# Layer 2's score products for the exponentials: four heads together, one key block by one query block

## The reference

```python
q = (x @ Wq).reshape(b, t, H, D)            # H = 16 heads, D = 64 = 32 "nope" + 32 rope
kv = kv_latent @ Wkvb                       # latent of 16 numbers per position
k = concat(kv, rope(k_rope))                # the rope part is one for all heads
v = concat(kv, zeros)
att = softmax(where(causal, q @ k.T / sqrt(D), -inf))
y = att @ v
x = x + y @ Wo
```

## Time and profile before

| | |
|---|---|
| median of 3 runs | 669.34 us (667.24 to 671.93) |
| profiled execution, its own time | 671.58 us |
| its span in the trace | 669.9 us |
| PE busy | 580.0 us (87%) |
| PEld busy | 342.0 us |
| DVE busy | 403.6 us (60%) |
| ACT busy | 311.2 us (46%) |
| POOL busy | 211.8 us (32%) |
| mean granted TensorE clock | 0.928 |

### The profile page before, as it was taken

One profiled execution on the slowest core, in us unless ns is written; L12 is line 12 of the kernel. 1 busy time (PEld: TensorE's weight loads), 2 busy tenths in 40 slices (PEclk: granted clock), 3 DMA queues, 4 the chain that ended last, 5 costly groups with the idle time before them and its releaser, 6 DMA issues.

```text
span 669.9 us, 10427 instructions
## 1 busy us (share of the span) xinstructions
PE 580.0 (87%) x3801; PEld 342.0 (51%) x3826; DVE 403.6 (60%) x932; ACT 311.2 (46%) x589; POOL 211.8 (32%) x276
## 2 busy tenths in 40 slices
PE   3884999887979899899978998999999998999873
PEld 1732444434434465555435555655676556654732
DVE  6374887676675655665675576756656764544362
ACT  2311756575453763456435545644445441553221
POOL 4562453242442622551252111405222002211101
PEclk9675999999988899899888999999999999999787
DMA  9322113111353433201570122225305020000000
GB/s 260 103 94 93 41 49 112 55 58 60 119 119 58 104 91 126 114 34 64 96 191 33 55 49 48 43 71 143 70 10 104 18 42 1 18 2 0 1 16 16
DMA packets 26658, 46.57 MB, mean 70 GB/s; under 512 B 3216, under 2 KB 12336, under 8 KB 26032
## 3 DMA queue, kind: packets, MB, share of 16 engines
q1 hardware_dynamic: 26608, 45.91, 25.0%
HBM read 27.62 MB, written 17.83 MB: 68 GB/s over the span
## 4 chain that ended last, share of the span: by engine, by line
PE 61%; DVE 15%; SPq 6%; DMA 5%; ACT 5%; issue 4%; POOL 4%; POOLq 0%; DVEq 0%; ACTq 0%
PE ps L541 13%; PE ps L605 11%; PE ps L509 10%; PE ps L483 6%; DVE NM L1098 4%; PE ps L485 4%; PE ps L480 3%; PE ps L507 3%; PE ps L726 2%; PE ps L655 2%; DVE stats L1082 2%; PE ps L549 2%; SPq L432 2%; DMA KS<-scr_k 1%; PE ps L588 1%
## 5 line engine op out<-in xcount | busy, mean ns | idle before, releaser
L1098 DVE TENSOR_REDUCE NM<-ps 128x1 f32<-128x512 f32 (+3 forms) x352 | 219.0, 637 | 126.6 <-PE ps L485 119.5
L764 ACT ACTIVATE PA<-ps 128x512 f32<-128x512 f32 x256 | 146.2, 595 | 148.7 <-PE ps L509 76.4
L509 PE MATMUL ps<-QS,K 128*128 128x384 f32 (+3 forms) x512 | 122.6, 353 | 0.0
L485 PE MATMUL ps<-maskb,identb 128*128 128x128 bf16 x512 | 111.1, 235 | 0.0
L509 PEld LDWEIGHTS ps<-QS,K 128*128 128x128 f32 x512 | 80.9, 191 | 39.7 <-issue 20.4
L1054 POOL TENSOR_SCALAR_AFFINE_SELECT PA<-PA 128x512 f32<-128x512 f32 x96 | 59.9, 637 | 123.8 <-ACT PC L768 123.3
L483 PE MATMUL ps<-K,QS 96*128 96x256 f32 (+3 forms) x256 | 88.2, 389 | 9.5 <-DVE NM L1098 9.2
L480 PE MATMUL ps<-KS,QS 96*128 96x256 bf16 (+3 forms) x256 | 74.2, 325 | 24.7 <-DVE NM L1098 16.4
L541 PE MATMUL ps<-PA,V 128*32 128x512 f32 (+2 forms) x768 | 80.1, 491 | 8.5 <-POOL PA L1054 7.6
L1012 POOL TENSOR_TENSOR whole<-terms 128x512 f32<-128x512 f32 x28 | 35.6, 1271 | 107.4 <-DVEq L1191 105.8
L957 POOL TENSOR_TENSOR rstd<-ve,half 128x4 f32<-128x4 f32 x20 | 20.4, 1020 | 154.6 <-DVE ve L1090 119.2
(11 more groups left out here) (156 smaller groups left out, 726.4 us busy)
## 6 DMA issues: line engine op xcount, KB each, us to landing
scr<-QC SPq DMA_DIRECT2D x24, 512.0 KB, 2.9
QS<-scr SPq DMA_DIRECT2D x32, 256.0 KB
QS<-scr_q SPq DMA_DIRECT2D x16, 288.0 KB
KS<-scr_k SPq DMA_DIRECT2D x16, 288.0 KB
QS<-scr SPq DMA_DIRECT2D x64, 64.0 KB
scr_k<-room SPq DMA_DIRECT2D x20, 128.0 KB, 1.9
scr_q<-room SPq DMA_DIRECT2D x12, 128.0 KB, 1.9
x<-in_x SPq DMA_DIRECT2D x4, 256.0 KB, 6.5
```

The source lines that it names most:

```text
L485: return pe.matmul(dst[:, P * (k - 1):P * k], identb[:], maskb[:, 0, :], start=False, stop=True)
L509: mm = pe.matmul(dst, keys[:, SEQ[n] % 2, q0:q0 + P], QS2[:, h, q0:T], start=(keys is K1), stop=(keys is K2))
L764: act.activation(PA[:, h % 8, T * k:T * k + T], ps[:, ST0 + (u + k) % 3, :], ACT.Exp, scale=scale)\
L1098: dve.tensor_reduce(dst, src, AX.X, ALU.max, negate=True).then_inc(fill_read, 1)
```

## The change

Layer 2's units become one pair (key block j, query block i) for the four heads of the group at once: two products of 512 columns (K1 and K2), whose moving operand is four pieces of 128 queries, one per head, 512 elements apart in QS2 (`scores_t2`). There are ten pairs with j at or below i, so there are still ten units; `BLOCKS2` takes the four diagonal ones first. Layer 1's units keep their shape (`scores_t1`).

The tiles PA and PC become one tile PG of two halves with ten places of 512 elements; `unit_place` says where a unit's exponential goes. In layer 2 the places are ordered so that for one head and one key block the query blocks lie 512 elements apart, and `values` reads its moving operand in 4, 3, 2 or 1 pieces of 128; its columns and its count are those of before. `values` waits once more, for all ten exponentials, and in layer 2 for all four causal instructions of its group.

POOL's causal instructions of layer 2 (`causal_blocks2`) are now one for each diagonal unit, 128 x 512 in one piece, stand at place (n, 2) instead of (n + 1, 0), and each waits only for its own unit's exponential.

The diff, without the views of constants that share the tile's memory:

```diff
@@ -40,6 +40,17 @@
 UNITS = 10
 
 CAUSAL_ORDER = (0, 1, 2, 3)
+
+BLOCKS2 = ((0, 0), (1, 1), (2, 2), (3, 3), (0, 1), (0, 2), (0, 3), (1, 2), (1, 3), (2, 3))
+PLACE2 = (0, 4, 7, 9)
+
+
+def unit_place(layer, c):
+    if layer == 2:
+        j, i = BLOCKS2[c]
+        return PLACE2[j] + i - j
+    hh, k = 2 * (c // 5) + (c % 5) // 2, (c % 5) % 2
+    return 8 + c // 5 if c % 5 == 4 else 2 * hh + k
 
 
 PHASES = ((1, 0), (1, 1), (1, 2), (2, 0), (1, 3), (2, 1), (2, 2), (2, 3))
@@ -262,8 +273,7 @@
         MRest = sb("MRest", [P, NT, HG])
         MF = sb("MF", [P, NT, 2, HG], F32R)
         MP = sb("MP", [3 * HG, 2, T])
-        PA = sb("PA", [P, 8, 2 * T])
-        PC = sb("PC", [P, 4, 2, 256])
+        PG = sb("PG", [P, 2, UNITS, T])
         OT = sb("OT", [P, T])
         rec = sb("rec", [P, NT, HG])
         ON1 = sb("ON1", [P, NT, H * D1])
...
@@ -500,14 +509,17 @@
                     mm = products(bank[:, w * j:w * j + w], n, h - heads + 1 + j, 3 - i, 4 - i)
                 mm.then_inc(score_fill, 1)
 
-            def scores_t(dst, n, h, j):
+            def scores_t1(dst, h, j):
 
                 q0 = P * j
-                if LAYER[n] == 1:
-                    return pe.matmul(dst, KS1[:, h, q0:q0 + P], QS1[:, h, q0:T], start=True, stop=True)
+                return pe.matmul(dst, KS1[:, h, q0:q0 + P], QS1[:, h, q0:T], start=True, stop=True)
+
+            def scores_t2(bank, n, j, i):
+
+                heads = slice(HG * (n % G), HG * (n % G) + HG)
                 for keys in (K1, K2):
-                    mm = pe.matmul(dst, keys[:, SEQ[n] % 2, q0:q0 + P], QS2[:, h, q0:T], start=(keys is K1),
-                                   stop=(keys is K2))
+                    mm = pe.matmul(bank.rearrange("p (h q) -> p h q", h=HG), keys[:, SEQ[n] % 2, P * j:P * j + P],
+                                   QS2[:, heads, P * i:P * i + P], start=(keys is K1), stop=(keys is K2))
                 return mm
 
             def scores_for_exp(n, hh, i):
@@ -519,27 +531,37 @@
                 if u >= 3:
                     pe.wait_ge(exp_done, u - 2)
                 bank = ps[:, ST0 + u % 3, :]
-                tiles = (((0, T, h, 0),), ((0, 3 * P, h, 1), (3 * P, T, h, 3)), ((0, 256, h - 1, 2), (256, T, h, 2)))[i]
-                for lo, hi, head, j in tiles:
-                    mm = scores_t(bank[:, lo:hi], n, head, j)
+                if LAYER[n] == 2:
+                    mm = scores_t2(bank, n, *BLOCKS2[u % UNITS])
+                else:
+                    tiles = (((0, T, h, 0),), ((0, 3 * P, h, 1), (3 * P, T, h, 3)),
+                             ((0, 256, h - 1, 2), (256, T, h, 2)))[i]
+                    for lo, hi, head, j in tiles:
+                        mm = scores_t1(bank[:, lo:hi], head, j)
                 mm.then_inc(st_ready, 1)
 
             def values(n, j):
 
-                pe.wait_ge(causal, NT * n + CAUSAL_ORDER.index(j) + 1)
+                pe.wait_ge(causal, NT * (n + 1) if LAYER[n] == 2 else NT * n + CAUSAL_ORDER.index(j) + 1)
                 if j == 0:
+                    pe.wait_ge(exp_done, UNITS * (n + 1))
                     if n:
                         pe.wait_ge(on_ready, n)
                     if n % G == 0:
                         pe.wait_ge(v1_ready if LAYER[n] == 1 else v2_ready, SEQ[n] + 1)
                 for hh in range(HG):
                     h = HG * (n % G) + hh
-                    slot = h % 8
-                    p = (PA[:, slot, 0:T], PA[:, slot, T:T + 3 * P], PC[:, slot // 2, hh % 2, :],
-                         PA[:, slot, T + 3 * P:2 * T])[j]
-                    v = V1[:, j, h, :] if LAYER[n] == 1 else V2[:, SEQ[n] % 2, j, :]
-                    mm = pe.matmul(ps[32 * hh:32 * hh + 32, BK_O, P * j:T], v, p, start=(j == 0), stop=(j == NT - 1),
-                                   skip_group_check=True)
+                    out = ps[32 * hh:32 * hh + 32, BK_O, P * j:T]
+                    if LAYER[n] == 1:
+                        v = V1[:, j, h, :]
+                        p = (PG[:, n % 2, 2 * hh, :], PG[:, n % 2, 2 * hh + 1, 0:3 * P],
+                             PG[:, n % 2, 8 + hh // 2, 256 * (hh % 2):256 * (hh % 2) + 256],
+                             PG[:, n % 2, 2 * hh + 1, 3 * P:T])[j]
+                    else:
+                        v = V2[:, SEQ[n] % 2, j, :]
+                        out = out.rearrange("d (i q) -> d i q", q=P)
+                        p = PG[:, n % 2, PLACE2[j]:PLACE2[j] + NT - j, P * hh:P * hh + P]
+                    mm = pe.matmul(out, v, p, start=(j == 0), stop=(j == NT - 1), skip_group_check=True)
                 if j == NT - 1:
                     mm.then_inc(pv, 1)
 
@@ -752,20 +774,15 @@
         def _(act):
             def main(n, hh):
                 if 0 <= n < NG:
-                    h = HG * (n % G) + hh
                     u = n * UNITS + 5 * (hh // 2) + 2 * (hh % 2)
                     scale = (D1 if LAYER[n] == 1 else D2) ** -0.5
                     if hh == 0 and n >= 2:
                         act.wait_ge(pv, n - 1)
                     if n <= 1 and hh == 0:
                         act.wait_ge(consts_ready, WCO if n else CONSTS)
-                    for k in range(2):
+                    for k in range(2 + hh % 2):
                         act.wait_ge(st_ready, u + k + 1)
-                        act.activation(PA[:, h % 8, T * k:T * k + T], ps[:, ST0 + (u + k) % 3, :], ACT.Exp, scale=scale)\
-                           .then_inc(exp_done, 1)
-                    if hh % 2:
-                        act.wait_ge(st_ready, u + 3)
-                        act.activation(PC[:, (h % 8) // 2, :, :].rearrange("p a t -> p (a t)"), ps[:, ST0 + (u + 2) % 3, :],
+                        act.activation(PG[:, n % 2, unit_place(LAYER[n], (u + k) % UNITS), :], ps[:, ST0 + (u + k) % 3, :],
                                        ACT.Exp, scale=scale).then_inc(exp_done, 1)
                 if hh == 2 and 1 <= n <= NG:
                     act.wait_ge(pv, n)
@@ -1043,20 +1060,28 @@
                 pool.wait_ge(q_low, c + 1)
                 pool.sem_inc(job_done[j], 1)
 
-            def causal_blocks(n):
-                s0 = HG * (n % 2)
+            def causal_blocks1(n):
+                pair = PG[:, n % 2, 0:8, :].rearrange("p (h k) t -> p h k t", k=2)
+                both = PG[:, n % 2, 8:10, :].rearrange("p a (b t) -> p a b t", b=2)
+                pool.wait_ge(exp_done, UNITS * (n + 1))
                 for j in CAUSAL_ORDER:
-                    blocks = (PA[:, s0:s0 + HG, 0:P], PA[:, s0:s0 + HG, T:T + P], PC[:, s0 // 2:s0 // 2 + 2, :, 0:P],
-                              PA[:, s0:s0 + HG, T + 3 * P:2 * T])[j]
-                    if j == CAUSAL_ORDER[0]:
-                        pool.wait_ge(exp_done, UNITS * (n + 1))
+                    blocks = (pair[:, :, 0, 0:P], pair[:, :, 1, 0:P], both[:, :, :, 0:P], pair[:, :, 1, 3 * P:T])[j]
                     heads = [[0, 2], [0, 2]] if j == 2 else [[0, HG]]
                     pool.affine_select(blocks, blocks, pattern=[*heads, [1, P]], compare_op=ALU.is_ge, fill=0.0, base=0,
                                        channel_multiplier=-1).then_inc(causal, 1)
 
+            def causal_blocks2(n):
+                for c in range(NT):
+                    blocks = PG[:, n % 2, unit_place(2, c), :].rearrange("p (h q) -> p h q", h=HG)
+                    pool.wait_ge(exp_done, UNITS * n + c + 1)
+                    pool.affine_select(blocks, blocks, pattern=[[0, HG], [1, P]], compare_op=ALU.is_ge, fill=0.0, base=0,
+                                       channel_multiplier=-1).then_inc(causal, 1)
+
             def main(n, hh):
-                if hh == 0 and 1 <= n <= NG:
-                    causal_blocks(n - 1)
+                if hh == 0 and 1 <= n <= NG and LAYER[n - 1] == 1:
+                    causal_blocks1(n - 1)
+                if hh == 2 and 0 <= n < NG and LAYER[n] == 2:
+                    causal_blocks2(n)
 
             clear(pool.memset(half[:], -0.5), HALF)
             clear(pool.memset(QS1[64:P].bitcast(F32), 0.0), QUERY_ZEROS)
```

11 lines of the change are left out of this document (5 added, 6 removed).

## The result

The changed kernel takes 656.83 us (median of four executions, 656.21 to 657.91); the kernel before, beside it on the same chip, 668.29 us (four, 666.68 to 671.93). The ratio is 0.985, with a 95% interval of 0.981 to 0.989: faster by 1.5%, 11.5 us. The profiled execution took 656.71 us, with a span of 655.0 us. Counted as a gain, 11.5 us, it lies just inside: the low end stood for 12.3 us off the median of 669.34.

What follows compares the result with a forecast made beforehand. The prediction took PE's own instruction stream to bound layer 2. It summed 3.9 us from shorter units and fills and 1.5 us from POOL's waits to 5.4 us off the median of 669.34, giving 664 us, range 657 to 673.

Steps and rivals of the forecast that it cites:

- What bounds the kernel: PE's own instruction stream sets layer 2's pace (61% of the chain); gains come only from overhead beside columns and waits.
- Units and fills: Layer 2 on PE: shorter units save 3.5 us, fills behind them 1.9; 0.73 on the path gives 3.9 us.
- Jumps: Layer 2's moving operands get 1344 jumps between pieces: taken as 0, at most 2.9 us.
- Rival 3: Jumps in layer 2's moving operands cost more than weight loads show: slower, 677 or even 718 us; chance 0.14.
- POOL's new place: Causal instructions at (n, 2) delay side stages behind them: counted as nothing, at most 2.5 us a place without cover.
- rival 4: POOL's new place makes side stages late at n = 14, 25 and 29: 7.5 us lost, 671 us; chance 0.06.
- POOL's waits, 1.5 us: PE's waits for POOL's causal instructions before the values of n = 21 (1.09) and n = 28 (0.37) vanish: 1.5 us.
- rival 2: PE's gain turns into layer-2 fills waiting for DVE (9.2 us before, mark 13): only 1.5 left, 668 us; chance 0.12.
- rival 5: Side stages come sooner and PE's other waits shrink: gain of 8 to 12 us, near 659; chance 0.14.
- The sum: Whole kernel: 3.9 us on PE plus 1.5 from POOL's waits, 5.4 us off the median of 669.34.

Runs made afterwards that it cites:

- units_only: The changed kernel with POOL's causal instructions of layer 2 back at place (n + 1, 0), each behind all ten exponentials: 660.76 us, ratio 0.990 to the kernel before.
- before_again: The kernel before, run again with no edit: 667.52 us, ratio 0.999.
- three_and_one: The changed kernel with all ten layer-2 units cut into widths of 384, 384, 128 and 128 columns: 668.62 us, ratio 1.001 to the kernel before.
- two_heads: The changed kernel with each layer-2 unit as four products of 256 columns instead of two of 512: 657.74 us, ratio 0.986 to the kernel before.
- one_piece: The changed kernel with each moving operand in one piece, same columns, other numbers computed: 657.67 us, ratio 0.987 to the kernel before.
- element_pieces: The changed kernel with the moving operand of layer 2's score products read in pieces of one element, 2048 bytes apart: 667.96 us, ratio 1.002 to the kernel before.
- lna_waits: The changed kernel with POOL's addition of stage lna, sequence 3, held until DVE has divided group 20: 655.86 us, ratio 0.984 to the kernel before.
- before_pool_waits: The kernel before with POOL's one rope-tile subtraction made to wait for DVE's variance of sequence 2: 664.50 us, ratio 0.996 to the kernel before.
- restored_pause: The changed kernel with three DVE statistics instructions repeated for sequence 2 (0.66 us expected): 662.36 us, ratio 0.993 to the kernel before.

## Why the prediction was right or wrong

**What bounds the kernel: right.** PE has 60% of the chain and 58.53 of 60 us in the stretch; the gain came from PE's overhead beside the columns and from its waits, as said.

**Units and fills: right, 3.9 us forecast.** A unit was to take 0.55 us and takes 0.54 to 0.56; the 384-column fill was to follow in 0.19 and follows in 0.18. In units_only, which has the units alone, the stages at full clock are shorter than before by 0.3 (n = 12), 0.2 (n = 15), 2.6 (n = 20 to 28), 0.1 (n = 29, against before_again's 20.32) and 0.3 us (n = 30, 12.88 to 12.61): 3.5 us together, with n = 13 and n = 14 left out. three_and_one gives the 2.5 us of n = 20 to 28 back and 4.3 more, having the short product in all ten units instead of four. The reason given, that a 128-column product can't hide a float32 load, is what tells three_and_one from two_heads.

The size given with it is not the one that counts. The forecast set a load's 191 ns against the products, and by that the 256-column products of two_heads would cost too. What a product has to cover, as the starts above show it, is the 108 ns between two such loads. That is also where the forecast misread the figure that it weighed and left out. The Trainium skill ("TensorE: Matmul & The Clock Gate", section on LDWEIGHTS) has 107 ns for 128 columns, which is short of the 191 ns that a float32 load lasts here but agrees with the 108 ns between two starts. It is longer than the 60 ns of a 128-column product, so by it too the short products cost some 0.05 us each, and not "about nothing".

**Jumps: right, 0.** one_piece has the same lengths. Rival 3 is out for pieces of 128 elements. It would have held for pieces of one: with element_pieces' 0.04 us for a product, the 2.5 us won in n = 20 to 28 turn into a loss of 3.0.

**POOL's new place: right for what it looked at, wrong that it costs nothing.** In 15 of the 16 groups the last causal instruction ends ahead of the group's last exponential, by 1.9 to 13.6 us; in group 22 it ends 0.75 us behind, 3.4 us before the values start. None of POOL's norm chains starts on a causal instruction's end, so rival 4 is out. But the forecast looked at POOL's own queue alone. At n = 27 the moved instructions run beside small DVE instructions and hold them, which costs 0.29 us.

**POOL's waits, 1.5 us: wrong.** The failed sentence is that "the exponentials, for which alone the values wait now, were done earlier". The values wait for `on_ready` too, and a wait for several semaphores shows only its last releaser. The row of the kernel before that I had not held against it is DVE's:

```profile
417.84 0.41 DVE L1148 TENSOR_TENSOR room<-ps,rec 128x256 f32<-128x256 f32 x1
```

The division ended at 417.84 + 0.41 = 418.25, POOL's first causal instruction at about 418.5 (417.85 and half of 1.23): of the 1.09 us only some 0.2 were POOL's causal instruction alone. Between units_only and the kernel after the move took 1.10 - 0.96 = 0.14 us off this wait and all 0.36 off the one at n = 28, and with what it did at n = 21, 22, 26, 27 and 30 about 0.6 us in all: less than half of the 1.5. lna_waits shows that the rest of the wait at n = 21 hung on POOL after all, but on its addition, which held DVE's subtraction for 1 us.

**DVE's waits: as said for rival 2, which is out.** L492 waits 10.2 us for DVE, below the 13 that the forecast put as the mark.

**What was missing: a held DVE instruction and the clock behind it, 2.5 to 4.3 us at n = 13.** The sum went by full-clock rows and had no term for the granted clock, though the profiled execution stood 99 us at half of it. A DVE instruction held by POOL's made a pause on PE of 1.66 or 1.85 us, and a half-clock stretch of 3.4 or 6.8 us began there. Of the 2.5 to 4.3 us, 0.6 to 0.8 are the shorter wait and 0.2 is left between before_pool_waits (24.33) and after (24.12); the rest, 1.7 to 3.4, is the clock's. In the new kernel DVE's instruction came 0.2 us sooner and POOL's subtraction 0.7 to 1.0 us later in the stage, and both pause and stretch went. This is rival 5 in size (near 659, chance 0.14) and in part in kind: "PE's other waits shrink", but through the clock rather than by DVE's work coming sooner. before_pool_waits and restored_pause show in both directions that the overlap makes the pause and that the stretch comes and goes with it. That the change would part the two instructions could not be read from its plan: this part of the gain is luck, and the range reached down to 657 only for a rival of which the forecast itself says that no row shows it.

**The sum.** At full clock the change took 0.3 us (n = 12), 0.2 (n = 15), 2.5 (n = 20 to 28), 0.4 (n = 29, 20.32 to 19.88) and 0.6 (n = 30): 4.1 us, 3.5 by the units and the rest by POOL's move, where the forecast had 5.4. n = 14 gave 0.6 more, whose cause is open, and n = 13 gave 2.5 to 4.3: 7.2 to 9.0 of the 9.2 to 11.5 us measured. The rest lies in half-clock stretches. n = 29 gave 1.5 us more where before has one there. Between one of the two profiles of before and one of the two of after, layer 1 gave -0.3 to 3.6 us and n = 31 0.3 to 4.1. The stretches' place and length change between executions of the same kernel, but the changed kernel has fewer: a median of 74.7 us at half clock in its ten executions against 86.5 in 75 of before. n = 13 makes 3.4 or 6.8 us of that. What makes the others rarer stays open: three_and_one and element_pieces, as slow as the kernel before, have medians of 76.5 and 76.0 us.

## What to carry to other kernels

Keep each product at least as long, from its start to the next, as the distance between the starts of two loads in a row (0.11 us here for float32, not the 191 ns that a load lasts), and read that distance from the trace by type; how many products the columns are cut into then hardly matters. Before a wait is counted as gained, look up when every other semaphore of the same wait came. When an instruction moves on one engine, look at what it now runs beside on the others. Where the granted clock falls behind a pause of PE, a gain of tenths of a microsecond can be worth microseconds, or cost as many: list the places where the clock falls, and what the engine waited for just ahead of each.

## What the runs showed of the hardware

- A small DVE addition, subtraction, cast or product with a constant between SBUF operands that runs beside a POOL instruction can be held until that one ends: 0.17 us became 0.86 or 1.05 (n = 13) and 0.96 (restored_pause), 0.16 became 1.20 (n = 21), 0.19 became 0.66 (n = 27); moved apart, the first two were 0.17 and 0.16 again. DVE's maxima, which read PSUM, lasted the same beside POOL (0.69 us for 512 columns), and so did its statistics (0.28) and reciprocals (0.18) of SBUF operands. The Trainium skill ("SBUF — State Buffer", Who interferes with whom) says that DVE and POOL share a pair of ports that one of them locks for a whole instruction: DVE instructions with two SBUF inputs against POOL instructions that read SBUF, and DVE instructions in a two-port mode. The trace agrees, with the numbers just given; the forecast had not used it.
- A float32 load of 128 x 128 lasts 191 ns, and behind 128-column products the next one starts 108 to 110 ns after it; a product of 128 columns takes 60 ns to the next start where no such load is in the way, one of 256 columns 118, of 512 columns 231.
- At n = 13 the granted clock fell behind pauses of PE of 1.48, 1.66, 1.85 and 2.49 us (three_and_one, before, before_again, restored_pause), for 3.4 or 6.8 us; after pauses of 0.97, 1.10 and 1.34 us at the same place (before_pool_waits, after, element_pieces) it stayed at 1.00. At n = 29 the same wait of 1.32 us had 3.4 us at half clock behind it in one execution and none in another.
- A moving operand in pieces of 128 elements costs nothing; in pieces of one element, 2048 bytes apart, 0.04 us for a product of 512 columns.
